# Attention and feed-forward on one core: the feed-forward product of each tile of rows made 15 periods later, from halves stored in memory

## The reference

```python
xn = layernorm(x)                              # x: 8 x 1024 x 512
q, k, v = xn @ Wq.T, xn @ Wk.T, xn @ Wv.T      # 16 heads of 32
cosh = 1 + 2 * |q - k|^2 / ((1 - |q|^2) * (1 - |k|^2))
att = softmax(-arccosh(cosh)) @ v              # per batch and head
w = int4_rounded(kernel)                       # 512 x 512
out = x + att @ Wo.T + (xn @ w + bias + (xn @ a) @ b)
```

## Time and profile before

| | |
|---|---|
| median of 3 runs | 2315.15 us (2313.09 to 2316.01) |
| profiled execution | 2314.24 us |
| its span, first to last instruction | 2312.4 us |
| granted TensorE clock, mean | 0.989 of 2.4 GHz |
| loop starts (first `distances`) | 137.4 us |
| busy share PE, DVE, ACT, POOL | 95%, 90%, 90%, 14% |

### The profile page before, as it was taken

How to read it: one execution, slowest core, us unless ns; L and a number is a source line. 1 busy time by engine, 2 the same in 40 slices (tenths; PEclk the granted TensorE clock), 3 DMA queues, 4 the chain that set the end, 5 groups by cost and what they waited for, 6 DMA issues and landing times.

```text
span 2312.4 us, 45533 instructions
## 1 busy us (share of the span) xinstructions
PE 2201.1 (95%) x17416; PEld 863.7 (37%) x17416; DVE 2083.9 (90%) x2794; ACT 2074.4 (90%) x1909; POOL 313.4 (14%) x193
## 2 busy tenths in 40 slices
PE   6999999999999999999999999999999999988886
PEld 2443333334343434434334433343433444322222
DVE  7779898999999999999999999999999999888987
ACT  4379999999999999999999999999999999999992
POOL 0101111111111111111111111111111111100003
PEclk9999999999999999999999999999999999999998
DMA  4354332534545343455425354453344543344433
GB/s 145 118 146 114 100 108 68 154 112 134 145 137 140 104 131 109 142 140 143 133 86 151 105 151 131 125 158 101 116 126 146 136 141 110 87 119 103 123 96 96
DMA packets 355428, 285.04 MB, mean 123 GB/s; under 512 B 81132, under 2 KB 294252, under 8 KB 355208
## 3 DMA queue, kind: packets, MB, share of 16 engines
q1 hardware_dynamic: 355208, 282.10, 43.0%
HBM read 159.77 MB, written 121.36 MB: 122 GB/s over the span
## 4 chain that ended last, share of the span: by engine, by line
PE 56%; ACT 19%; issue 11%; DVE 10%; SPq 2%; DMA 2%; POOL 1%; ACTq 0%; DVEq 0%; POOLq 0%
PE pM L305 20%; PE pU L225 12%; PE pO L237 11%; ACT root L529 9%; ACT root L535 8%; PE pZ L253 6%; DVE root L871 3%; DVE root L866 2%; PE pM L295 2%; ACT qk L556 1%; SPq L1112 1%; PE pM L278 1%; PE pO L305 1%; DVE kx L739 1%; PE pM L281 1%
## 5 line engine op out<-in xcount | busy, mean ns | idle before, releaser
L529 ACT ACTIVATE root<-pU 128x1024 f32<-128x1024 f32 x1008 | 1016.9, 1039 | 78.2 <-PE pU L225 72.8
L535 ACT ACTIVATE root<-root 128x2048 f32<-128x2048 f32 x512 | 989.5, 1933 | 46.0 <-DVE root L866 46.0
L866 DVE TENSOR_SCALAR root<-root 128x2048 f32<-128x2048 f32 (+1 forms) x512 | 647.0, 1264 | 71.5 <-ACT root L529 71.2
L225 PE MATMUL pU<-QS,KS 100*128 100x512 f16 x2048 | 610.6, 381 | 40.9 <-ACT root L529 37.2
L871 DVE TENSOR_TENSOR root<-root 128x2048 f32<-128x2048 f32 x256 | 586.2, 2290 | 1.0 <-PE pO L237 0.9
L237 PE MATMUL pO<-root,VX 128*32 128x512 f32 x4096 | 505.8, 607 | 7.8 <-ACT root L535 7.7
L1018 POOL TENSOR_TENSOR sqr<-qk 128x512 f32<-128x512 f32 x112 | 208.5, 1862 | 997.0 <-ACT qk L556 910.9
L225 PEld LDWEIGHTS pU<-QS,KS 100*128 100x128 f16 x2048 | 175.2, 98 | 384.0 <-issue 143.4
L253 PE MATMUL pZ<-root,ones 128*32 128x512 f32 x2048 | 269.3, 597 | 18.3 <-DVE root L871 18.3
L237 PEld LDWEIGHTS pO<-root,VX 128*32 128x32 f32 x4096 | 103.9, 109 | 283.9 <-issue 191.4
L1013 POOL TENSOR_TENSOR xts<-xts,bias_b 128x512 f32<-128x512 f32 x64 | 82.9, 1297 | 680.2 <-PE pM L295 622.9
(11 more groups left out here) (228 smaller groups left out, 2210.3 us busy)
## 6 DMA issues: line engine op xcount, KB each, us to landing
v_d<-v_o SPq DMA_DIRECT2D x64, 264.0 KB, 2.1
k_d<-kx SPq DMA_DIRECT2D x64, 264.0 KB, 2.1
KT<-k_d SPq DMA_DIRECT2D x64, 264.0 KB
VX<-v_d SPq DMA_DIRECT2D x64, 264.0 KB
xts<-in_x SPq DMA_DIRECT2D x32, 512.0 KB, 4.3
res_d<-f_o SPq DMA_DIRECT2D x64, 256.0 KB, 3.9
QS<-qh_d SPq DMA_DIRECT2D x128, 128.0 KB
KS<-kh_d SPq DMA_DIRECT2D x128, 128.0 KB
```

The costliest lines, as they stand in the source:

```text
L225: mm = pe.matmul(pU[:, col:col + HALF], KS[i][:, h, j * P:(j + 1) * P], QS[i][:, h, half * HALF:(half + 1) * HALF], start=True, stop=True)
L529: act.activation(root[:, q % RING, cols], pU[:, cols], ACT.Square).then_inc(squared, 1)
L535: act.activation(root[:, q % RING, :], root[:, q % RING, :], ACT.Sqrt).then_inc(rooted, 1)
L866: v.tensor_scalar(root[:, q % RING, cols], root[:, q % RING, cols], CS * CS, CS * CS, ALU.max, ALU.subtract).then_inc(clamped, 1)
```

## The change

1. The f product leaves the place behind its projections. With `F_LAG` = 7, tile m = p - 7 is multiplied in period p (`feed`), 15 periods after period m - 8 had its projections. Its halves are written to a new DRAM tensor `xT_d` (`store_xT`) when they are made, and read back into `fT` (`load_feed`), together with the rows of x (`xr`), which are now also read again. The prologue therefore has no f product, no `take_f` and no add of the bias, and periods 0 to 6 have none either.
2. Tiles 56 to 63 are fed in the periods of their own number, at k = 0, 1, 2, beside tile p - 7 at k = 12 to 14 (m up to 55). So the last 8 periods hold 15 f products, which they didn't before.
3. The preparation of Wf goes from the prologue into periods 0 to 4, on DVE (`largest_of` twice, `quantise` in three steps, `fold` in four), with `high` on ACT in period 3; the four low-rank matmuls of PE go into periods 1 and 2. That of Wo moves from periods 1 to 3 to periods 4 to 6.
4. `xT` and `xt` have two buffers instead of three. The banks of the prologue are fixed by purpose instead of rotating.
5. `take_o` adds the f result that is still in SBUF (`xr`) instead of one that SP has read back; `load_res`, `load_res_last` go.
6. `load_three` is issued by GpSimd instead of SP, with its own store of the divisors. On SP it stood behind the 16 issues of `pass_kv(62)`.
7. At the end `add_pair(QUADS - 1)` stands ahead of `divide(56)`, and `divide_two` waits for that division.

```diff
+F_LAG = LEAD - 1
...
+            def feed(m, b, first, last):
+                late = m >= NT - LEAD
+                t = xT[m % 2] if late else fT[m % 2]
+                if first == 0 and late:
+                    pe.wait_ge(fT_late[m % 2], ((m - NT + LEAD) // 2 + 1) * 16)
...
+                elif k in (0, 1, 2):
+                    if k == 0:
+                        pe.wait_ge(taken["o"], o)
+                        pe.wait_ge(feat_split[1], NT)
+                    feed(p, 0, 4 * k, 4 * k + 4)
...
-                if n >= 2:
+                transpose_feat(n, 0, 2)
+                if n:
-                    project(n - 1, "f", (u + 2) % 4, 0, 12)
...
             add_pair(QUADS - 3)
             clamp(QUADS - 1)
+            add_pair(QUADS - 1)
             divide(56)
-            add_pair(QUADS - 1)
             divide_last()
...
+            def load_three():
+                blk, groups = NB - 1, KC - 1
+                rows = rz_d[blk * H:blk * H + groups * G4, :]
+                g.wait_ge(xn_done, NT)
+                g.wait_ge(feat_stored, NT // 2 * 64)
+                g.wait_ge(att_stored, 32 * (PERIODS - 2))
+                g.dma_start(raw3, ...).then_inc(raw3_loaded, 16)
+                g.wait_ge(divisors, NB - 1)
+                g.dma_start(rows..., zc[0:P - P // KC, 1, :]).then_inc(rz3_stored, 16)
+                g.wait_ge(rz3_stored, 16)
+                for h in range(G4):
+                    g.dma_start(rzb3[h * HD:(h + 1) * HD, :, :], src).then_inc(raw3_loaded, 16)
...
+                if n == NT - 1 and k == 15:
+                    load_feed(NT - LEAD)
+                    load_feed(NT - LEAD + 1)
+                if n > NT and k == 5 and p + 1 < PERIODS:
+                    load_feed(p + 1)
```

More of the change, by code:

```diff
@@ L312, in project, with low_rank_rows @@
                     mm.then_inc(made[k], 1)
+            def feed(m, b, first, last):
[3 more added lines that the diff above has]
+                    pe.wait_ge(fT_late[m % 2], ((m - NT + LEAD) // 2 + 1) * 16)
+                elif first == 0:
+                    pe.wait_ge(fT_loaded[m % 2], (m // 2 + 1) * 16)
+                if m == 0 and first == 0:
+                    pe.wait_ge(w_low, 4)
+                mm = product(pM[b], lambda c: t[:, 0, c, :], lambda c: t[:, 1, c, :], W["f"], first, last)
+                if last == 3 * KC:
+                    mm.then_inc(made["f"], 1)
+            def low_rank_rows(c, b):
+                if c == 0:
+                    pe.wait_ge(rank_loaded, 2 * 16)
+                pe.matmul(pM[b][:, :], At[:, c * P:(c + 1) * P], Bl, start=True, stop=True).then_inc(low_rank, 1)
             def output(o, b, first, last):
@@ L416, in keys @@
                 key_sums(p, 1)
[L419 to L423 removed]
+            pe.wait_ge(small_loaded, 16)
+            transpose_x(0, 5)
             for n in range(LEAD):
[L425 removed]
                 pe.wait_ge(x_split, n + 1)
@@ L600, in scalar_program @@
             high(0, "q", 0)
-            high_x(0, 3)
+            high_x(0, 5)
             high(1, "k", 1)
@@ L897, in behind @@
                         aug_rows(n)
-                if k == 0 and p and n - 1 < NT:
-                    take_f(n - 1, 1)
+                if k == 0 and 1 <= m <= NT - LEAD:
+                    take_f(m - 1, 1)
+                if k == 4 and n >= NT:
+                    take_f(p, 0)
                 if o >= 0:
@@ new lines, in load_feed @@
+            def load_feed(m):
+                rows, i = slice(m * P, (m + 1) * P), m % 2
+                if m < NT - LEAD:
+                    there = min(m + F_LAG + LEAD + 1, NT)
+                    for parity in range(2):
+                        sy.wait_ge(xT_stored[parity], (there + 1 - parity) // 2 * 16)
+                    if m >= 2:
+                        sy.wait_ge(made["f"], f_place[m - 2] + 1)
+                    sy.dma_start(fT[i][:, :, :, :].rearrange("p s c n -> p (s c n)"), xT_d[rows, :]).then_inc(fT_loaded[i], 16)
+                    if m >= 2:
+                        sy.wait_ge(taken["o"], m - 1)
+                        sy.wait_ge(f_stored, f_place[m - 2] * 16 + 16)
+                    sy.dma_start(xr[:, i, :], x[rows, :]).then_inc(xr_loaded[i], 16)
+                else:
+                    for parity in range(2):
+                        sy.wait_ge(xT_stored[parity], NT // 2 * 16)
+                    sy.wait_ge(made["v"], NT)
+                    if m >= NT - LEAD + 2:
+                        sy.wait_ge(made["f"], f_place[m - 2] + 1)
+                    sy.dma_start(xT[i][:, :, :, :].rearrange("p s c n -> p (s c n)"), xT_d[rows, :]).then_inc(fT_late[i], 16)
+                    sy.wait_ge(xT_made, NT)
+                    sy.wait_ge(summed, 2 * NT)
+                    if m >= NT - LEAD + 2:
+                        sy.wait_ge(featT_made[0], NT)
+                        sy.wait_ge(featT_made[1], NT)
+                        sy.wait_ge(k_stored, NT * 16)
+                        sy.wait_ge(v_stored, NT * 16)
+                    if m >= NT - LEAD + 2:
+                        sy.wait_ge(xb_done, f_place[m - 2] + 1)
+                    sy.dma_start(res_last[m - NT + LEAD], x[rows, :]).then_inc(xr_late[i], 16)
```

467 lines of the change are left out of this document (239 added, 228 removed).

## The result

Before: 2315.58 us median of 4 runs (2313.09 to 2316.86). Changed: 2298.19 us median of 4 (2294.45 to 2304.41). The ratio is 0.9932, 95% interval 0.9915 to 0.9949. The forecast was 2304 with 2290 to 2315, and faster by over 0.2% at 0.80. The execution profiled after the change is the slowest of its four (2304.41, span 2302.6). Against the profiled one of before (2314.24, span 2312.4) it is 9.8 us shorter, where the sum of the forecast said 10.5.

A forecast was written before the change was run, and what follows sets the result against it. No single bound (PE 95%, DVE 90%, ACT 90%), so stages were summed: -30 + 4.5 + 0 + 21.5 (periods 56 to 63) - 6.5 = -10.5 us, giving 2303.7 from the profiled execution; forecast 2304, range 2290 to 2315.

The forecast's parts named there:

- Prologue, -30: Prologue: without f product and take_f, tiles 2 to 7 take 10.4 us each, -27.5; tile 0 -2.3; together -30.
- Periods 0 to 7, +4.5: Periods 0 to 7: later stack load, Wf's preparation and PE's relief sum to +4.5 us, from -3 to +12.
- (a): Period 0, step 7: the first stack's second half comes later relative to the loop's start, +2.5 us.
- (c): Periods 0 to 7: seven f products leave PE; gain bounded by 4.5 us, taken as 3.
- (b): Early periods: Wo's preparation, costing 7.5 us, only moves; Wf's comes as well and costs 5 us.
- Periods 8 to 55, 0: Periods 8 to 55: PE's, ACT's and DVE's lists unchanged, loads issued well ahead; 0, and 3 us either way.
- Late periods, +20.0: Periods 56 to 62: added f products cost +4.7 in period 56, +3.1 per even and +2.0 per odd period.
- The argument from PE's quarters: Odd late periods: first and fourth quarter become as full as the third, 7.8 us each, giving 29.8 us per period.
- rival B: Periods 56 to 63: products cost nearly full length, about +25, GpSimd's adds slowing DVE +8; 2315; 0.13 with another rival.
- Rival A: Periods 56 to 63: PE's free time takes the late products almost whole, +5 to +10; 2288 to 2293; chance 0.25.
- Tail, -6.5: Tail: GpSimd's own loads and the earlier last pair together bring -6.5 us, from -10 to +2.
- Both named terms: Tail: divisors' store and loads issued by GpSimd, -4 us; last pair ahead of divide(56), -2.5 us.

The follow-up runs named there:

- e4: Changed kernel plus matmuls with unread results, 3 per prologue tile and 12 in each of periods 3 to 6; 2302.58 us (one run).
- e5: Changed kernel with four waits removed: deviation of tiles 8 and 9, Wo's magnitude, tile 56's halves, late read-backs; 2291.31 us, 0.9902 of before.
- e7: Changed kernel, VectorE's and GpSimd's adds for the 15 late f products cut to 8 of 512 columns, last GpSimd division without its new wait; 2291.4 us.
- e9: Changed kernel with one matmul per late f product and both engines' adds cut to 8 columns, the change's tail kept; 2282.16 us (one run).
- e11: Changed kernel with only GpSimd's bias adds for the 15 late f products cut to 8 of 512 columns; 2281.8 us (one run).
- e10: e5 with the last pair added behind division 56; 2291.13 us, 0.9909 of before.
- e3: Changed kernel with 11 of 12 matmuls left out of the f products at k = 0 to 2 of periods 56 to 63; 2298.36 us (one run).
- e2: Changed kernel with the divisors' store and the three groups' loads issued by SP again, at k = 13 of period 62; 2304.31 us (one run).
- e1: Changed kernel with the last pair added behind divide(56) again, as before the change; 2295.92 us (one run).
- e8: Changed kernel, one matmul per late f product, pair behind the division, last GpSimd division without its new wait; 2287.92 us (one run).

## Why the prediction held, and which steps did not

**Prologue, -30 against -32.5.** The mechanism was right: with the f product gone, `take_f`'s wait for PE no longer delays the second sum of squares, and a tile is 10.20 or 10.80 us, where 10.4 was said. The missing 2.5 us are mostly in tile 1, which the sum left out: it ran from 35.3 to 47.5 in before and runs from 31.6 to 41.8 now, 2.0 us less. Tile 0 gained 2.8 instead of 2.3, and it started 0.9 us earlier, which is scatter (16.7 here, 18.4 in e4); tiles 2 to 7 gained 26.8 of the 27.5. e4 bears out that PE's 9.5 us do not set the tile. The forecast's lower bound of -33 was added up wrongly: with 9.5 us a tile and tile 0's 2.3 it is -35.

**Periods 0 to 7, +4.5 against +1.3.** (a) The stack load's wait was right in kind and in e5 shows with 3.55 us, but in the change it lies behind ACT's wait for the deviation, which I had not followed through ACT's list. (c) PE's relief was booked with a gain of 3 and is worth nothing in periods 3 to 6 (e4). (b) Most of Wf's preparation lies in periods 1 to 3, which take 98.6 us against 97.0 without any: 1.6, and not 5. That Wo's "only moves" was wrong too. In periods 4 to 6 it costs 5.1 us (103.6 against 98.5), where it had cost 7.5. Period 0 adds 1.5 and period 7 0.6; period 0 alone scatters from 30.4 to 33.3 where its code is the same.

**Periods 8 to 55, 0 against +6.0.** Shown to be no steady cost of the change: the same list gave 1627.6 to 1636.4 us, and odd and median even periods are as long as before. Whether the change makes TensorE's stops more frequent is open, since before has one trace. The bound of 3 us either way was too narrow, and took no account of stops that before itself shows twice.

**Late periods, +20.0 against +21.3 for periods 56 to 62.** This is the step that was right only in its sum. The three odd periods were to cost 2.0 each and cost 0.6 (28.4, with 27.8 before). The three even ones were to cost 3.1 each and cost 4.6 (31.8, 37.4 and 31.4, where before had 29.6, 28.9 and 28.3). The argument from PE's quarters holds for PE's share: with no other delay (e7) an odd period is 28.4 and period 58 is 29.5, and with short products (e9) 27.3 and 28.4, so the products cost 1.1 us a period, 7 in six. (The odd mean moved by 0.6 alone because one of before's three, period 61, has a clock of 0.94 and 28.6 us.) As large a part or larger, 7 to 9 us by e11, is rival B's mechanism, GpSimd's adds slowing VectorE's division, which stood at nothing in the sum and, in the rival, beside every product; it bites only in even periods. Around the start of period 60 VectorE's wait of 5.33 us for the load of `zc` comes on top (1.79 in before); e5's move of the feed's loads did not reliably shorten it (3.06 there, 5.76 in e10). Period 56 was +4.7 and is +5.8. The granted clock had no place in the forecast, and it moves single periods by about a microsecond (e3). Rival A, that PE's free time takes the products, is near the truth for PE alone and wrong for the total. So it is partly luck that the sum of this stage came out within 1.3 us.

**Tail, -6.5 (and +1.5 for period 63) against -5.9.** Both named terms fail. GpSimd's own loads bring 0 to -3 instead of -4 (e2), and the pair's place costs 2.2 instead of bringing 2.5 (e1). What brings the gain is that GpSimd's division of the last two no longer runs beside VectorE's division 56: 31.38 us in before, 25.3 in e1 and e8. Part of these 6 us is the granted clock, which in before is at its lower level for 3.5 us of the stretch (from 2288.7) and in e1 never. The forecast had the separation as a subordinate clause without a price of its own, although show the cast at 2.51 us beside GpSimd. Pair, wait and clock together turned 31.38 into 27.55, 3.8 us where 2.5 were forecast. Whether the wait that the change adds, or only the later start of that division, would have done it in before's own tail was not tried alone.

On the Trainium skill ("GPSIMD Engine Reference", Specifications): its rule that GpSimd shares its SBUF interfaces with VectorE bears on both places, and the trace agrees, with 0.69 against 1.66 us for one cast. The Trainium skill's page "DMA: Bandwidth & Descriptors" (Anatomy of one DMA) gives its 2 us for a DMA of GpSimd and no figure for one of SP. So the forecast's "some 2 us longer than SP's" does not follow from it. Measured, GpSimd's chain is 10.3 to 12.0 us and SP's 10.2 and 10.5, between nothing and 1.8 us longer.

## What to carry to other kernels

When work moves off the critical engine, list what its helpers do at the new place: here GpSimd's adds of 1.3 to 1.7 us, beside a division on VectorE, cost at least as much over six periods as the products' 2.6 us of matmuls on TensorE. With three engines near 90%, a cut on any of them may free the same microseconds, so test them one at a time and together before adding terms. When a test leaves matmuls out, compare the granted clock before the times: in e3 it took back most of what the cut had saved. Moving a wait pays only if what fills the freed time does not delay the next engine, so follow the list of every engine, not just that of the one that waited.

## What was not expected of the hardware

Beside GpSimd's tensor operations a 128x2048 clamp took 4.12 us (1.22 alone), a 128x512 cast 2.08 (0.43) and a 100x128 copy 2.54 (0.23 in before). The 128x2048 product of roots took 2.29, as alone, where it started 0.2 us ahead of GpSimd's subtraction (2245.72), and it was the subtraction that took 5.03. In before it started 0.9 us behind the same subtraction (2263.04, 3.95 us):

```profile
2263.96 5.17 DVE L871 TENSOR_TENSOR root<-root 128x2048 f32<-128x2048 f32 x1
```

In e2 it took 5.34, started 0.3 us behind GpSimd's division (2251.11). In these rows the instruction that starts second is the long one.

And TensorE can stop for up to 2.1 us in a row of short matmuls with nothing to wait for, in some executions and not in others, at times with 3.5 us at the lower clock behind it. This moves this kernel's time by up to 9 us.
